# GpSimd clears a scratch tile ahead of each group of gathers in a four-layer graph network

## The reference

```python
h = relu(layernorm(x)); x = x + L0(h)   # relu(segment_sum((h @ W[type])[src] * w, dst))
h = relu(layernorm(x)); x = x + L1(h)   # Y = relu(h[src] @ Mh + edge64 @ Mx + b); relu([h, segment_sum(Y, dst)] @ U + ub)
h = relu(layernorm(x)); x = x + L2(h)   # segment_sum((h @ W2[type])[src], dst)
h = relu(layernorm(x)); x = x + L3(h)   # sums of h[dst] + edge16 @ We + be over src, an MLP, a layer norm
```

## Time and profile before

| what | value |
| --- | --- |
| median of three runs | 26590.07 us (26584.51 to 26607.13) |
| the profiled execution | 26739.13 us |
| its span | 26737.3 us |
| POOL busy | 15584.5 us, 58% |
| DVE busy | 10909.5 us, 41% |
| PE busy | 9422.0 us, 35% |
| ACT busy | 2485.9 us, 9% |
| granted TensorE clock, mean | 0.524 of full speed |

### The profile page before, as it was taken

One profiled execution on the slowest core, in us unless ns is written; L12 is line 12 of the kernel. 1 busy time (PEld: TensorE's weight loads), 2 busy tenths in 40 slices (PEclk: granted clock), 3 DMA queues, 4 the chain that ended last, 5 costly groups with the idle time before them and its releaser, 6 DMA issues. The chain is left out here.

```text
span 26737.3 us, 230656 instructions
## 1 busy us (share of the span) xinstructions
PE 9422.0 (35%) x48147; PEld 7349.2 (27%) x48149; DVE 10909.5 (41%) x38508; ACT 2485.9 (9%) x7729; POOL 15584.5 (58%) x16453
## 2 busy tenths in 40 slices
PE   1555555433333333333333443333332111111266
PEld 0222222223333332323233333333331111111154
DVE  7555565533333334333333433232224333333374
ACT  5000000000000000000000100000001222222200
POOL 1555656666666665666666356666665666666500
PEclk7555555555555555555555565555555555555586
DMA  2222222222222222222222222222222222222262
GB/s 84 77 76 78 78 78 72 60 55 54 54 54 54 54 53 43 54 53 54 53 54 54 50 97 54 54 54 53 54 54 56 69 69 69 69 68 68 75 222 92
DMA packets 1019636, 1785.28 MB, mean 67 GB/s; under 512 B 366838, under 2 KB 475667, under 8 KB 1019078
## 3 DMA queue, kind: packets, MB, share of 16 engines
q1 hardware_dynamic: 498838, 1127.77, 13.7%
q0 software_dynamic: 513696, 654.80, 10.4%
q10 hardware_dynamic: 7056, 2.21, 0.0%
HBM read 1279.37 MB, written 510.79 MB: 67 GB/s over the span
## 5 line engine op out<-in xcount | busy, mean ns | idle before, releaser
L909 POOL DMA_INDIRECT arena<-table,arena x6464 | 6131.2, 949 | 3208.6 <-issue 3177.9
L999 PE MATMUL psum<-arena 128*128 128x64 f32 x19392 | 4492.9, 420 | 9646.4 <-issue 3312.6
L999 PEld LDWEIGHTS psum<-arena 128*128 128x128 f32 x19392 | 4268.0, 329 | 9871.6 <-issue 9869.9
L952 DVE TENSOR_TENSOR arena<-arena,psum 128x64 f32 x9696 | 2154.2, 222 | 9221.0 <-remote 3172.3
L685 POOL DMA_INDIRECT rec<-arena x3125 | 2991.9, 957 | 2490.8 <-issue 1955.4
L1097 POOL DMA_INDIRECT rec<-arena x3232 | 3187.8, 986 | 1942.9 <-DVE arena L1115 1014.1
L909 POOL DMA_INDIRECT arena<-ptable,arena x3232 | 3167.3, 980 | 1554.3 <-issue 1541.9
L928 DVE TENSOR_SCALAR arena<-arena 128x128 f32<-128x128 f32 x9696 | 2260.8, 321 | 280.5 <-issue 279.9
L462 PE MATMUL psum<-arena 128*128 128x196 bf16 (+1 forms) x4375 | 1378.0, 428 | 2274.5 <-DVE arena L593 1260.7
L1177 PE MATMUL psum<-arena 128*128 128x192 bf16 x3232 | 584.2, 361 | 4079.1 <-DVE arena L1115 1985.2
L1112 DVE CAST arena<-psum 128x384 bf16<-128x384 f32 x1616 | 786.8, 550 | 2236.2 <-remote 2225.5
(11 more groups left out here) (187 smaller groups left out, 10114.3 us busy)
## 6 DMA issues: line engine op xcount, KB each, us to landing
arena<-rec SPq DMA_DIRECT2D x1616, 352.0 KB
arena<-rec SPq DMA_DIRECT2D x440, 488.0 KB
arena<-in_edge SPq DMA_DIRECT2D x625, 232.0 KB
arena<-table,arena POOLq DMA_INDIRECT x6464
rec<-arena POOLq DMA_INDIRECT x6357
table<-arena SPq DMA_DIRECT2D x196, 512.0 KB
arena<-ptable,arena POOLq DMA_INDIRECT x3232
rec<-arena SPq DMA_DIRECT2D x198, 244.0 KB
```

Source lines behind the costliest of these rows:

```text
L909: nc.gpsimd.indirect_dma_start(rows[q][:, j * D:(j + 1) * D], None, tab, bass.IndirectOffsetOnAxis(ap=idx[:, j, field:field + 1], axis=0)) ...
L952: v.tensor_tensor(block_sum, block_sum, ps[q][:, j * D:(j + 1) * D], ALU.add).then_inc(s_add[j], 1)
L999: last = nc.tensor.matmul(ps[q][:, j * D:(j + 1) * D], hot[q][:, j * P:(j + 1) * P], rows[q][:, j * D:(j + 1) * D], start=True, stop=True)
```

## The change

In `gather_layer` GpSimd gets six more tiles of G * P = 1024 fp32 columns, one for each place of the ring, and six semaphores. In each group, after its waits and before its eight indirect DMAs, it clears the tile of that place to zero. The memset counts up its semaphore, and GpSimd waits at the same place of the next turn for the memset of the turn before. Nothing reads the tiles. The assertion says that they end below x.

```diff
@@ -873,7 +873,9 @@
     recs, rows, hot = ([b.take(G * n) for _ in range(RG)] for n in (RW, D, P))
-
+    spare = [b.take(G * P) for _ in range(RG)]
+    assert b.at <= ARENA - NB * D
+    s_pause = [sem(f"{name}_pause{q}") for q in range(RG)]
     s_ld, s_g, s_hot, s_mm, s_sum, s_msg = ([sem(f"{name}_{n}{q}") for q in range(RG)] for n in ("ld", "g", "hot", "mm", "sum", "msg"))
@@ -904,7 +906,10 @@
                     pool.wait_ge(s_ld[q], i * 16 + 16)
 
                     wait_earlier(pool, s_mm[q], i)
+                    wait_earlier(pool, s_pause[q], i)
                     pool.sem_inc(s_begun)
+
+                    nc.gpsimd.memset(spare[q], 0.0).then_inc(s_pause[q], 1)
                     for j in range(G):
                         nc.gpsimd.indirect_dma_start(rows[q][:, j * D:(j + 1) * D], None, tab,
```

## The result

| | kernel before | kernel after |
| --- | --- | --- |
| median (lowest to highest), 7 runs each | 26584.51 us (26574.35 to 26607.13) | 26665.97 us (26645.73 to 26683.06) |
| ratio, 95% interval | | 1.003 (1.002 to 1.004) |
| profiled execution | 26739.13 us | 26673.5 us |

A forecast was written before the change was run, and what follows sets the result against it. GpSimd's issuing (10.0 us a group) plus stalls (1.5) was taken to bound the gathers. Savings of 185 and 125 us, less 30 for bursts, gave -280 us: 26590 to 26310 us, range 25970 to 26850.

The forecast's parts named there:

- something shared is overrun by a DMA every 1.25 us: Gathers: each indirect DMA needs about 1.40 us of an unnamed shared thing; other engines queue until GpSimd falls silent.
- TensorE is late because VectorE is: Gathers: GpSimd waits for TensorE to free a row buffer, and TensorE for VectorE's eight adds, sometimes 1.4 us apart.
- the stall is 1.1 us plus 0.15 us per DMA: GpSimd's stalls in the gathers: 5.97 us after 32 DMAs, 7.31 after 40, 10.65 after 64; 1.1 us for stopping and restarting.
- longer runs between stalls save 0.23 us a group: First and third gather: a group takes 11.3 us instead of 11.53, saving 185 us over 808 groups.
- rival (b): Gathers: the whole stall is the shared thing's rate, 1.44 us a DMA; pauses come out of stalls, 26590 us; chance 0.18.
- The memset's price: GpSimd, each group: 1.05 us taken, 0.96 from the iota's rate, 0.53 from below, 1.26 with another DMA gap.
- the 30 us for memsets that meet VectorE's bursts: Gathers: taken off the 310 us saving because VectorE's one-hot bursts might hold up GpSimd's memsets.
- The second gather: Issuing with the memset takes 11.30 us, hardly a stall left; 11.35 instead of 11.66 us a group, 125 us saved.
- Rival (a): Gathers: backlog and stalls vanish, GpSimd's issuing is the bound; saves 610 us, 25980 us; chance 0.13.
- Rival (c): Gathers: the memset keeps the backlog standing, stalls stay and every memset is added, 1270 us; 27860 us; chance 0.12.
- Rival (d): Gathers: the memset exceeds the 1.5 us available; at 2.0 us it costs 635 us more, 27220 us; chance 0.07.
- The sign: Whole kernel: faster had chance 0.63, within 0.2% of no change 0.18, slower 0.19.

The follow-up runs named there:

- chips A to C: Labels for the chips of the earlier runs; the kernel before took 26585 us in the result, then 26652, then 26385 and 26398 us.
- D and E: Chips of the last runs; the unchanged kernel before took 23091 and 23159 us; on the second the kernel after took 24012.02 us, ratio 1.0368.
- twice the pause: Kernel after with a memset of 2048 columns instead of 1024, in three tiles used in turn: 26899.78 us, ratio 1.0091 to before.
- light kernel: Kernel before without one-hots and adds, one matmul of eight per group, ScalarE doing nothing; record loads and indirect DMAs unchanged: 25996.96 us, ratio 0.9856.
- six of eight: Kernel before with six of each group's eight indirect DMAs, one-hots, matmuls and adds unchanged: 23052.19 us, ratio 0.8734.
- ScalarE's copies: Kernel before with 16 unread one-column copies on ScalarE per group in the first and third gather: 26700.02 us, ratio 1.0018.
- the one comparison: Kernel before with eight one-hots per group replaced by one 1024-column comparison in the second and third gather: 26366.35 us, ratio 0.9989.
- the light kernel with the pause: The light kernel plus the change's 1024-column memset ahead of each eight indirect DMAs: 25734.99 us, ratio 0.975 to before.

## Why the prediction was wrong

- **What bounds the gathers.** Right that GpSimd's issuing plus stalls is the whole time, and that something shared is overrun by a DMA every 1.25 us. It is met only on chips A to C; on D and E the same issuing meets no limit. The prediction took the stalls for a property of the kernel, on the sole ground of one trace and 149 us between two times. Which thing it is, and whether chips or hours differ (D and E also came last), stays open.
- **What ends a stall.** Right that GpSimd waits for the semaphore of TensorE's matmuls of six groups ago. Wrong that "TensorE is late because VectorE is": these matmuls had ended 14 to 56 us before GpSimd went on, in each of the 298 stalls over 3 us, and without the chain of adds the stalls stay. What is late is the count.
- **The step that failed** is "the stall is 1.1 us plus 0.15 us per DMA, and the 1.1 us is the price of stopping and restarting". It came from the first five stalls, of which three were of 40 DMAs. From it followed that longer runs between stalls save 0.23 us a group. The runs show no such saving in this kernel: with 512 and 1024 columns stalls are fewer and shorter by just the memsets' time, and the silence of the first gather stays at 1590 us. What holds on chips A to C is a rate of 1.43 to 1.46 us per DMA, rival (b), whose objection (0.187 falls to 0.166 us per DMA) was read from too few rows. The whole first gather of before has 53 stalls after 32 DMAs, of 5.56 us in the mean less the 0.30, and 35 after 40, of 7.34 us: 0.174 and 0.184 us per DMA. From one to the other the share rises and doesn't fall; only the single stall after 64 is lower, and eight stalls after no more than 8 DMAs, of 4.59 us, fit neither reading. So the trace of before didn't bear a price of stopping of 1.1 us.
- **The memset's price.** The row, 0.96 forecast, is 0.968. In its place in the queue it costs 0.85 us on chip A and 0.83 on E, not the 1.05 taken and far from the 1.26 of the upper bound: the gap behind it shrinks. This size didn't matter where the stalls absorbed it; on chip E 1212 memsets would have cost 1273 instead of 1007 us, ahead of what the second gather gave back. Of the 30 us for memsets that meet VectorE's bursts no row shows anything on GpSimd: the memsets' rows are 952 to 979 ns. The prediction's other reading, by which the 30 us would be 0 since the two leave each other alone, was wrong too: the memsets hold up VectorE's one-hots (last section).
- **The second gather.** 4585 us forecast, 4701 measured on A: the same failed step. That its stretched DMAs (980 ns) would stay was wrong in part: 973 on A, and 949 on E.
- **Rival (a)**, GpSimd's issuing as the bound at 10.98 us a group, is what chip E does (10.85), but there the kernel before does 10.03, so it is a loss. **Rival (c)**, the memset isn't rest, fell with twice the pause: no stall left. **Rival (d)** is right in its mechanism: at 2048 columns (11.70 us a group) the excess over 11.53 counts. The loss of 858 us on chip E goes (c)'s way for another reason: there are no stalls to pay from.
- **The sign.** 0.3% slower had 0.19 of the chance with other mechanisms. Within (b) I had a time of exactly before's; that a pause taken from idle time can only be free or cost something, never pay, should have tipped the sign. That the measured time lies inside the stated range, 25970 to 26850, is no merit of the forecast's mechanism: the range was drawn wide enough to take in (b).

Left open: what the limit is, and so what delays the counts; why the pause pays in the light kernel in two gathers of three; and the 5 ns or so that each other instruction seems to add per DMA (light kernel 1.392 us, kernels with all of before's work 1.429, six of eight 1.445, all on chip C, at some 2, 10 and 13 other instructions per DMA, a fit of three points; ScalarE's copies on chip B cost 48 us for 12928, 3.7 ns each). No version that keeps all of the computation is more than 0.1% faster than before: the one comparison gains that on chip C, and on chip D the same edit costs 1.2% more (1.0779 against 1.0655, both with 1536 columns). Before is the fastest of the kernels run on D and E.

## What to carry to other kernels

A stall that the profile can't name may be the chip's or the hour's and not the kernel's: profile the same kernel on a second chip and at another time before building on it, and prefer an edit that costs nothing where the stall is absent. A filler on the engine that sets the pace is at best free, when it fits in idle time, and costs its full start-to-start time (here 0.83 us, not the 0.97 of its row) as soon as it doesn't. Where an engine waits for a semaphore, compare the end of the work behind it with the time at which the count is recorded: here that alone tells a late engine from a late count. Look for two-input VectorE instructions that start just ahead of an indirect DMA: having the DMA start 0.3 us ahead of the add, and not 0.06 us behind it, was worth 0.46 us each time.

## What the runs showed of the hardware

- On chip E GpSimd keeps up an indirect DMA every 1.25 us for 4 ms on end; the time on chip D (23091 us) fits the same. In the result and on B and C the first gather held no less than 1.427 us per DMA with the matmuls at work, whatever the rows (64 or 128) and bytes, and 1.392 with almost nothing beside it; only the light kernel with the pause got to 1.352.
- In the runs with stalls a semaphore's count is recorded as much as 55 us after the matmuls that make it, and the engine that waits for it goes on only then. With a group every 11.70 us, or on chip E, the adds of the first and third gather follow their matmuls after 0.15 us.
- In the runs with stalls the other engines' small instructions come 1.4 us and more apart, as L957 and the matmul at 5581.14 do above; on chip E the same adds stay in one piece, 2.77 us for eight:

```profile
6404.87 2.77 DVE L952 TENSOR_TENSOR arena<-arena,psum 128x64 f32 x8 [5.10 <-PE psum L999]
6407.56 2.14 DVE L928 TENSOR_SCALAR arena<-arena 128x128 f32<-128x128 f32 x8
6415.02 2.77 DVE L952 TENSOR_TENSOR arena<-arena,psum 128x64 f32 x8 [5.31 <-PE psum L999]
```

- A GpSimd memset of fp32 costs 0.82 ns a column in the queue, between 1024 and 1536 columns, and a VectorE burst beside it doesn't lengthen it (952 to 979 ns over 1212 rows). The memset does hold VectorE up. The one-hots on chip E, before and after (min/median/max ns), and one of them beside a memset:

```profile
L928 DVE TENSOR_SCALAR arena<-arena x9696: 267/294/583, 4497.3 to 17457.4; 128x128 f32<-128x128 f32 x198
```

```profile
L933 DVE TENSOR_SCALAR arena<-arena x9696: 267/296/1823, 4497.0 to 18316.0; 128x128 f32<-128x128 f32 x198
```

```profile
5481.44 1.72 DVE L933 TENSOR_SCALAR arena<-arena 128x128 f32<-128x128 f32 x1
5482.10 0.98 POOL L912 MEMSET arena<- 128x1024 f32 x1
```

On chip E 291 one-hots take over 0.6 us, 1.71 in the mean, and in the result 362, of 1.47 us; before the change there is none. Each of them lies beside a memset and ends 0.08 to 0.15 us after it. It cost no time here, since VectorE doesn't set the pace.
